# Message passing in three edge blocks on one Trainium2 core: blocks of 11, 13 and 10 tiles, and 160-column sum products in the third

## The reference, cut to what matters

```python
x = x + gnn_0(layernorm(x), ...)       # x is 256 x 512
x = x + ffn_0(layernorm(x), ...)       # 16 experts
x = x + gnn_1(layernorm(x), edge_attr, path_coeffs, src, dst, path_indices)
x = x + ffn_1(layernorm(x), controller, f1, f2)

def gnn_1(x_nodes, x_edges, path_coeffs, src, dst, path_indices):
    x1 = x_nodes[src].reshape(-1, 16, 32)      # 4352 edges, 16 segments of 32
    x2 = x_edges.reshape(-1, 16, 32)
    i1, i2, i3 = path_indices.T                # 64 paths
    contrib = path_coeffs[None, :, None] * x1[:, i1, :] * x2[:, i2, :]
    edge_out = zeros(4352, 16, 32).at[:, i3, :].add(contrib)
    return zeros(256, 512).at[dst].add(edge_out.reshape(-1, 512))
```

## Time and profile before

| | us |
|---|---|
| median of 3 runs | 276.04 |
| lowest, highest | 275.96, 276.04 |
| the profiled execution, its own time | 276.05 |
| span from its first to its last instruction | 274.2 |
| PE busy | 262.2 (96% of the span) |
| DVE busy | 223.6 (82%) |
| ACT busy | 168.5 (61%) |
| chain that ended last, share by engine | PE 83%, DVE 9%, ACT 2% |

### The profile page before, as it was taken

The page is one execution under the profiler, slowest core; times in us unless marked ns, Lnnn a source line. Parts: engine busy times, 40 slices in busy tenths (PEclk is TensorE's granted clock), DMA queues, the critical chain, the costliest instruction groups (busy, mean ns, idle before and its releaser), DMA issues.

```text
span 274.2 us, 5661 instructions
## 1 busy us (share of the span) xinstructions
PE 262.2 (96%) x1631; PEld 185.1 (67%) x1639; DVE 223.6 (82%) x662; ACT 168.5 (61%) x341; POOL 39.5 (14%) x52
## 2 busy tenths in 40 slices
PE   6899999999999899998999999989999989999996
PEld 4566798886444799996778786756665654478633
DVE  5977665299657999999999999999999987755272
ACT  6931341010526999978878787499999709443260
POOL 4000150060006766661000000000000000000000
PEclk9999999999999999999999999999999999999999
DMA  6699990000014765555342000014544439000002
GB/s 208 222 414 409 436 421 17 0 4 0 1 38 127 200 176 152 157 154 155 88 145 77 2 1 1 2 28 145 161 154 150 151 89 343 31 2 2 2 0 76
DMA packets 12592, 33.91 MB, mean 124 GB/s; under 512 B 3345, under 2 KB 3602, under 8 KB 12306
## 3 DMA queue, kind: packets, MB, share of 16 engines
q1 hardware_dynamic: 10482, 26.73, 27.1%
q0 software_dynamic: 2080, 6.82, 8.8%
HBM read 32.50 MB, written 1.05 MB: 122 GB/s over the span
## 4 chain that ended last, share of the span: by engine, by line
PE 83%; DVE 9%; issue 3%; ACT 2%; DVEq 1%; DMA 1%; ACTq 0%; SPq 0%
PE psum L1349 15%; PE psum L1296 14%; PE psum L1250 10%; PE psum L1352 8%; PE psum L1274 5%; DVE big L1041 4%; PE psum L1279 4%; PE psum L1302 3%; PE psum L1423 3%; PE psum L1449 3%; PE psum L1193 3%; PE psum L1179 2%; PE psum L1133 2%; PE psum L1340 1%; PE psum L1231 1%
## 5 line engine op out<-in xcount | busy, mean ns | idle before, releaser
L1296 PE MATMUL psum<-big,dst_oh 128*128 128x512 f32 x108 | 50.7, 594 | 0.5 <-DVE big L1041 0.5
L607 ACT ACTIVATE prod<-edges,coef_b 128x320 f32 (+1 forms) x78 | 43.8, 594 | 10.6 <-PE psum L1352 9.2
L1349 PE MATMUL psum<-prod,ident 128*128 128x128 f32 x160 | 32.1, 295 | 1.0 <-DVE prod L1031 0.9
L1349 PEld LDWEIGHTS psum<-prod,ident 128*128 128x128 f32 x160 | 24.5, 190 | 10.2 <-issue 9.4
L1031 DVE TENSOR_TENSOR prod<-big,prod 128x320 f32<-128x320 f32 (+1 forms) x53 | 29.1, 551 | 0.5 <-issue 0.3
L1296 PEld LDWEIGHTS psum<-big,dst_oh 128*128 128x128 f32 x108 | 18.7, 191 | 15.1 <-issue 14.3
L1250 PE MATMUL psum<-edges,big 128*128 128x256 f32 x128 | 28.3, 380 | 0.0
L607 ACT ACTIVATE xparts<-edges,coef_b 128x320 f32 (+1 forms) x48 | 26.1, 589 | 1.0 <-PE psum L1349 0.6
L1250 PEld LDWEIGHTS psum<-edges,big 128*128 128x128 f32 x128 | 24.1, 190 | 3.5 <-issue 0.3
L1041 DVE TENSOR_TENSOR big<-big,prod 128x64 f32 (+2 forms) x80 | 26.3, 329 | 0.0
L472 POOL DMA_INDIRECT big<-xn_rows,big x16 | 16.9, 1059 | 30.5 <-DMA xn_rows<-xn 23.5
(11 more groups left out here) (221 smaller groups left out, 525.1 us busy)
## 6 DMA issues: line engine op xcount, KB each, us to landing
big<-in_w SPq DMA_DIRECT2D x3, 2048.0 KB, 16.0
edges<-in_edge SPq DMA_DIRECT2D x1, 3584.0 KB, 23.9
edges<-in_f SPq DMA_DIRECT2D x7, 512.0 KB, 3.5
edges<-in_edge SPq DMA_DIRECT2D x1, 2560.0 KB, 23.4
edges<-in_edge SPq DMA_DIRECT2D x5, 512.0 KB, 3.6
edges<-in_f SPq DMA_DIRECT2D x1, 2560.0 KB, 9.8
big<-in_f SPq DMA_DIRECT2D x4, 512.0 KB, 3.6
big<-in_gnn_w SPq DMA_DIRECT2D x1, 1024.0 KB, 6.0
```

The costliest lines, as they stand in the source:

```text
L607: nc.scalar.activation(slot(n)[:, 0:BLOCKS[b], :], segment(edges_of(b), single_column(words, p)), ACT.Copy, scale=coef_b[:, p:p + 1]).then ...
L1296: last = mm(bank[2 + h], dst_oh[:, n % DR, h * P:(h + 1) * P], tile_sums(b, t), start=False, stop=False)
L1349: last = mm(path_sums(to), ident[:], product[:, 0:PT].rearrange("p t u -> p (t u)"), start=False, stop=True, skip_group_check=True)
```

## The change

- The blocks become 11, 13 and 10 tiles. In the first, `multiply` covers 11 tiles and `add` 3 (10 and 2 before); in the second 13 and 7 (14 and 8 before).
- In the third block PE sums 5 tiles in one product of 160 columns (4 tiles, 128 columns before), and DVE adds 5 (6 before). Three segments of 160 columns fit a bank, so the 16 segments take six banks (4, 5, 6, 7, 0, 1) and not four. The start of a segment's sums is worked out on PE's queue with a multiplication, a division and a remainder.
- The third block's `rest_sums` lie where the first block's gathered rows were, and ACT clears them (5 tiles) at paths 20, 26, 32, 38 and 44 of the second block.
- ACT copies all six banks of the second block after path 7 of the third (`LEAD = 8`).
- After the third block ACT copies six banks in one go, behind the parts of the first tile.
- `ctrl`, half of `f1` and one tile of `f2` take the room that the third block's sums had; the last stage's tensors start at the front of the big buffer.

```diff
-    BLOCKS = [10, 14, 10]
-    FIRST = [0, 10, 24]
-    KEPT = [8, 6, 4]
+    BLOCKS = [11, 13, 10]
+    FIRST = [0, 11, 24]
+    KEPT = [8, 6, 5]
     EARLY = [0, 0, 1]
     PT = 4
-    PT2 = [k - PT for k in KEPT]
+    PT2 = [k - PT for k in KEPT[:2]]
+    PER_BANK = 512 // (KEPT[2] * U)
-    LEAD, REST_LEAD = 6, 11
+    LEAD = 8
+    CLEAR_AT, CLEAR_EVERY = 20, 6
...
+        def last_sums(k):
+
+            b = psum[:].bitcast(mybir.dt.uint8).rearrange("p (s e) -> p s e", e=4 * U)
+            at = nc.s_assert_within((k * 171 + 2048) // 32 % 128, 0, 128 - KEPT[2],
...
+            return b[:, bass.ds(at, KEPT[2]), :].rearrange("p o e -> p (o e)").bitcast(F32)
...
-        kept_sums = [sum_room[0][:, 0:KEPT[0], :], x1g[1][:, 0:KEPT[1], :], sum_room[0][:, 0:KEPT[2], :]]
-        rest_sums = [sum_room[0][:, KEPT[0]:, :], sum_room[1], sum_room[0][:, KEPT[2]:, :]]
+        kept_sums = [sum_room[0][:, 0:KEPT[0], :], x1g[1][:, 0:KEPT[1], :], x1g[0][:, 0:KEPT[2], :]]
+        rest_sums = [sum_room[0][:, KEPT[0]:, :], sum_room[1], x1g[0][:, KEPT[2]:BLOCKS[2], :]]
...
-            return [4, 5, 6, 7] + list(range(PT2[b]))
+            return [4, 5, 6, 7] + list(range(PT2[b] if b < NB - 1 else 2))
...
             sp.wait_ge(mults, NP * (NB - 1))
+            sp.wait_ge(scattered, FIRST[1])
             sp.dma_start(ctrl_sb, rows(ctrl)).then_inc(ctrl_in, 16)
...
-                    if i < PT:
+                    if b == NB - 1:
+                        n = min(PER_BANK, NS - PER_BANK * i)
+                        nc.scalar.activation(
+                            kept_sums[b][:, :, PER_BANK * U * i:U * (PER_BANK * i + n)].rearrange("p t (k u) -> p k t u", u=U),
+                            bank[q][:, 0:n * KEPT[b] * U].rearrange("p (k t u) -> p k t u", t=KEPT[b], u=U), ACT.Copy)\
+                            .then_inc(block_out, 1)
+                    elif i < PT:
...
-                if b == 2 and p == 0:
-                    act.wait_ge(scattered, FIRST[1])
-                    for i in range(BLOCKS[b] - KEPT[b]):
-                        nc.scalar.activation(rest_sums[b][:, i, :], zero_b[:, 0:1].broadcast_to([P, D]), ACT.Copy)\
-                            .then_inc(cleared[b], 1)
+                if b == 1 and (p - CLEAR_AT) % CLEAR_EVERY == 0 and 0 <= p - CLEAR_AT < CLEAR_EVERY * (BLOCKS[2] - KEPT[2]):
+
+                    act.wait_ge(mults, NP)
+                    nc.scalar.activation(rest_sums[2][:, (p - CLEAR_AT) // CLEAR_EVERY, :], zero_b[:, 0:1].broadcast_to([P, D]), ACT.Copy)\
+                        .then_inc(cleared[2], 1)
...
                 if b == 2 and p == LEAD - 1:
-                    copy_sums(1, 0, PT)
-                if b == 2 and p == REST_LEAD - 1:
-                    copy_sums(1, PT, 8)
+                    copy_sums(1, 0, PT + PT2[1])
...
-                    last = mm(path_sums(to), ident[:], product[:, 0:PT].rearrange("p t u -> p (t u)"),
-                              start=False, stop=True, skip_group_check=True)
-                    if KEPT[b] > PT:
+                    if b == NB - 1:
+                        last = mm(last_sums(to), ident[:], product[:, 0:KEPT[b]].rearrange("p t u -> p (t u)"),
+                                  start=False, stop=True, skip_group_check=True)
+                    else:
+                        mm(path_sums(to), ident[:], product[:, 0:PT].rearrange("p t u -> p (t u)"),
+                           start=False, stop=True, skip_group_check=True)
                         last = mm(more_sums(b, to), ident[:], product[:, PT:KEPT[b]].rearrange("p t u -> p (t u)"),
                                   start=False, stop=True, skip_group_check=True)
                     last.then_inc(psums, 1)
```

More of the change, by code:

```diff
@@ L87, in more_sums @@
             return product_sums(psum[:, 0:NS * PT2[b] * U], PT2[b] * U, k)
+        def last_sums(k):
+            b = psum[:].bitcast(mybir.dt.uint8).rearrange("p (s e) -> p s e", e=4 * U)
+            at = nc.s_assert_within((k * 171 + 2048) // 32 % 128, 0, 128 - KEPT[2],
+                                    skip_runtime_bounds_check_because="three segments to a bank, six banks around the scatters")
+            return b[:, bass.ds(at, KEPT[2]), :].rearrange("p o e -> p (o e)").bitcast(F32)
         def carve(base, dt_size=4):
@@ L217, in graph_and_experts @@
         w_cat = take([KC, G + EX])
-        take = carve(x1g[0].rearrange("p t f -> p (t f)"))
+        take = carve(sum_room[0].rearrange("p t f -> p (t f)"))
         f1_parts = [take([KC // 2, f1.shape[1]])]
         ctrl_sb = take([KC, ES])
+        f2_mid = take([1, D])
         take = carve(edges[:, BLOCKS[0]:LATE, :].rearrange("p t f -> p (t f)"))
         f1_parts.append(take([KC // 2, f1.shape[1]]))
-        f2_lo = take([6, D])
+        f2_lo = take([5, D])
         f2_hi = carve(late)([FC - 6, D])
-        take = carve(big[:, BLOCKS[0] * D:])
+        take = carve(big[:, 0:(BLOCKS[0] + 2 * BLOCKS[1] - KEPT[1]) * D])
         xnT2 = take([KC, N])
@@ L321, in f2_sb @@
         def f2_sb(c):
-            return f2_lo[:, c, :] if c < 6 else f2_hi[:, c - 6, :]
+            return f2_lo[:, c, :] if c < 5 else f2_mid[:, 0, :] if c < 6 else f2_hi[:, c - 6, :]
         x_in, idx_in, w_in, w1_in, w3_in, w2_in = (sem(n) for n in
@@ L422, in _ @@
                     .then_inc(f1_in, 16)
-            for i in range(0, 6, 2):
-                sp.wait_ge(mults, NP * (NB - 1) + 44 + 3 * i)
-                sp.dma_start(f2_lo[:, i:i + 2, :], rows(f2)[:, i:i + 2, :]).then_inc(f2_in, 16)
+            for i, (to, lo, n) in enumerate(((f2_lo[:, 0:2, :], 0, 2), (f2_lo[:, 2:5, :], 2, 3), (f2_mid, 5, 1))):
+                sp.wait_ge(mults, NP * (NB - 1) + 44 + 6 * i)
+                sp.dma_start(to, rows(f2)[:, lo:lo + n, :]).then_inc(f2_in, 16)
             sp.wait_ge(mults, NP * NB)
@@ L1354, in _ @@
                     last.then_inc(psums, 1)
-                    if KEPT[b] > PT and b and p % 2 and p < NP - 1:
+                    if b == 1 and p % 2 and p < NP - 1:
                         mm(bank[4][:, 0:N], zero_b[:], iota_b, start=False, stop=True, skip_group_check=True)
```

## The result

The changed kernel takes **278.38 us** (median of 4 runs, 278.19 to 278.51) where the kernel before takes 276.03 on the same chip: 1.0084 times as long [1.0072, 1.0097], or +2.35 us.

A forecast was written before the change was run, and what follows sets the result against it. DVE was taken to bound all three blocks, PE close behind; 8.2 us more for PE less 6.6 to spare gives 1.6, the sum's 1.45 but for rounding: 276.05 + 1.45 = 277.5 us, range 276.4 to 278.7.

The forecast's parts named there:

- The bound moves to PE, which had 3.2 and 3.4 us to spare: Second and third blocks: DVE bounds before; 8.2 us of PE work and delay exceeds PE's 6.6 us to spare.
- Before the first multiply, +0.45: Start of the first block: a third indirect gather lands at 90.43, where DVE started at 89.98; bounds 0 and 0.6.
- First block, 38.9: DVE's 64 paths at 448 columns take 38.9 us against 35.49, +3.4 (3.1 to 4.3).
- The column line: DVE's price per path, 0.00105 us per column, from the second and third blocks; 0.603 at 448 columns.
- DVE in the second block: DVE needs 51.5 us from 129.3, ends at 180.8 and gives back the 4.3 the first block took.
- PE at the second block, 50.9: PE's sums and fillers 30.3 plus 12 scatters of 1.72, from 133.55 to 184.5; one scatter more than before.
- banks, 4.42: PE between second and third blocks: early scatter to first path 3.56 before, plus two more banks at 0.43, to 188.9.
- third block, 38.3: PE's 64 wider products 17.7 plus twelve scatters 20.6, ending at 227.2 against 225.75 before, +1.45.
- nearly free wide product: Rival for the third block: 160 columns cost PE little more than 128, 3.4 drops out; 275.1 us, chance 0.06.
- much slower: Rival: two register instructions per product hold PE's queue (282), or PE's clock falls to its lower level; chance 0.06.
- DVE's stop of about 2.5 us near multiply 136: Third block, path 8: ACT's six copies hold up its scaling and so DVE; costs nothing while PE ends later.
- The early clearing at nothing: Moving 5 x 0.6 us of ACT's clearing into the second block costs or gains nothing; DVE didn't wait for it before.

The follow-up runs named there:

- the first run: The changed kernel without the filler products between the sums of the second block: 276.6 us, 1.0023 against the kernel before.
- the run with two gathers: The changed kernel with two indirect gathers ahead of the first multiply instead of three, the first block's last tile not gathered: 277.45 us, 1.0047.
- the run with late gathers: The changed kernel with the third block's gathers issued in the second block, one every four paths, and no longer in the first: 278.12 us, 1.0069.

## Why the forecast was right in direction, and where it fell short

*The bound moves to PE, which had 3.2 and 3.4 us to spare.* Right. PE waits for no multiply in the second and third block, work taken from PE comes out of the time (the first run), a start delay passes through whole (the run with two gathers), and moving DVE's stop changes nothing (the run with LEAD 11).

*Before the first multiply, +0.45.* Too low: 90.84 - 89.98 = +0.86. DVE's wait for the rows ended at 90.51, as forecast (90.43). I set the first multiply at the landing. But DVE still works off register and semaphore instructions between the wait and the multiply, and that takes 0.34.

*First block, 38.9.* This is the step that failed most: 39.78. The column line gave 38.6, and it holds: the median distance between multiplies is 0.605, which times 64 is 38.7. What failed was the choice that the excess of 0.019 per path would shrink because it belongs to very short adds. In the trace before, it was mainly three stalls of DVE, 0.87 in all by the distance of the multiplies around them (the two in mid-block show as idle for 0.26 and 0.23), besides a distance a little above the line. After, the same three are there, 0.66 in all, and the long adds that a gather's start makes add 12 x 0.045 = 0.54, of which the run with late gathers took 0.3 away. The bound given for "the excess stays", 39.8, was the right value, but in part by luck: the long adds in it are new.

*DVE in the second block.* Its length was right (51.7 from 130.62 to 182.33, 51.5 forecast). The forecast said that it gives back the 4.3 that the first block took; by its own terms that was 0.45 + 3.4 = 3.9. Measured, the first block and its start took 130.62 - 125.47 = 5.2, and the second gave 4.1 back. PE was behind anyway.

*PE at the second block, 50.9; banks, 4.42; third block, 38.3.* Right: 50.87, 4.37, 37.99. A 160-column product takes 0.272 from start to start (the two ahead of the scatter at 190.66 take 0.55 from 190.11), against 0.276. The nearly free wide product was a wrong rival. The Trainium skill, page TensorE: Matmul & The Clock Gate, section Back-to-back issue gap, whose sustained rates stood behind the 1.1 us of that rival, doesn't hold for these float32 products: the widening cost 64 x (0.272 - 0.223) = 3.1 us. Neither form of "much slower" came either: with its second register instruction a product still starts every 0.272, and the granted clock is 1.00.

*DVE's stop of about 2.5 us near multiply 136.* It was 1.96, and the multiply came at 189.60 (188.5 forecast). It costs nothing, as forecast.

*The early clearing at nothing.* Wrong as a statement on the change, although no number of the sum hung on it. The forecast looked at whether anyone waited in the trace before; the new sizes would have made ACT's clearing late, which costs about 3.1 us more than the change does. As the clearing was part of the change, it was already in the forecast's ACT times.

*Behind the third block, 0.* Right.

## What to carry to other kernels

Before work is shifted off the busiest engine, the slack of the engine behind it has to be worked out stage by stage: here, by the forecast's prices, 6.6 us of slack met 8.2 us of new work and delay (nearer 9.0 by the time measured), and the time grew although the busiest engine lost work. A delay at the start of a stretch that another engine then bounds is passed on whole. When a block's mean stands above a line of price by columns, split the excess into stalls and slow instructions before assuming that it shrinks: stalls stay. And "nobody waits for it" is a statement on the kernel before; read it again with the new sizes.

## What the hardware did that was not expected

- An indirect gather of POOL was held up for 6.16 and 7.37 us, and in the run with late gathers for 8.90 and 16.94 in the second block; a held gather ended 0.82 us after DVE's next pause began (in the second block this was no more than an add and a multiply that don't overlap as the others do, at 141.60 and 165.88). Which gathers are held isn't explained: most in the same stream take 0.95. After a held one the next follow each other 1.25 us apart, and these are the ones that start together with a DVE add. No engine waited for their rows, but the long adds are on the path.
- A gather that starts within 0.004 us of a DVE add lengthens it from 0.245 to 0.29 us.
- Taking out a filler of 0.11 us on PE gave 0.056 back.
- From the end of the wait for a gather (90.51) to the first multiply behind it (90.84) took 0.34 us of DVE's own instructions.
